# Reading the rows of a scan step for the tensor engine: one full 128-row matmul in place of a 16-row block

## The reference

```
x = x + attention_layer(x, cond)      # B = 8, S = 1024, 512 features, 16 heads
x = x + scan_layer(x, cond)           # d_inner = 1024, d_state = 16

# scan_layer
xr, gate = split(x @ W_in.T);  xr += cond
xc = silu(causal_conv4(xr));   xn = layernorm(xc) * ln_g + ln_b
Bm, Cm, dt = split(xn @ W_xproj.T)
Ad = 1 + tanh(dt @ W_dt.T + b_dt) * 0.01 * (-tanh(A_log))
Bd = Bm * min(norm(xn), 1)
for t in range(S):                    # h: (B, 16, 1024)
    h = clip(h * Ad[t] + Bd[t] * xn[t], -10, 10)
    y[t] = sum over the 16 states of Cm[t] * h
y = (y + D * xn) * silu(gate) @ W_out.T
```

## Time and profile before

| | |
|---|---|
| median of 3 runs | 6766.6 us (6751.14 to 6771.64) |
| the profiled execution | 6754.87 us, span 6753.0 us |
| PE busy (matmul) | 6163.2 us, 91% |
| PE weight loads | 2592.1 us, 38% |
| DVE busy | 4561.2 us, 68% |
| ACT busy | 2370.0 us, 35% |
| POOL busy | 3208.9 us, 48% |
| mean granted TensorE clock | 0.929 of 2.4 GHz |

### The profile page before, as it was taken

The page is one execution under the profiler, slowest core; times in us unless marked ns, Lnnn a source line. Parts: engine busy times, 40 slices in busy tenths (PEclk is TensorE's granted clock), DMA queues, the critical chain, the costliest instruction groups (busy, mean ns, idle before and its releaser), DMA issues. The chain is left out here.

```text
span 6753.0 us, 73075 instructions
## 1 busy us (share of the span) xinstructions
PE 6163.2 (91%) x24000; PEld 2592.1 (38%) x24000; DVE 4561.2 (68%) x5829; ACT 2370.0 (35%) x4476; POOL 3208.9 (48%) x2625
## 2 busy tenths in 40 slices
PE   8999999999999999999855889999999999999997
PEld 3444444444444444444332323333333333333333
DVE  4655555655655655655336888888788888888883
ACT  2443434444444443434443323233232323233110
POOL 1766756757666676755622323324142333424212
PEclk7999999999999999999877779898999989899998
DMA  2223223133232323223032334434344343434433
GB/s 89 77 79 94 79 72 93 53 107 88 71 91 57 93 79 91 82 61 87 30 114 69 80 94 109 116 89 138 78 118 108 105 125 92 130 84 123 102 88 98
DMA packets 411563, 613.08 MB, mean 91 GB/s; under 512 B 58768, under 2 KB 190096, under 8 KB 410672
## 3 DMA queue, kind: packets, MB, share of 16 engines
q1 hardware_dynamic: 374320, 558.04, 30.0%
q10 hardware_dynamic: 36864, 50.38, 3.0%
HBM read 305.12 MB, written 201.38 MB: 75 GB/s over the span
## 5 line engine op out<-in xcount | busy, mean ns | idle before, releaser
L1103 POOL TENSOR_TENSOR acc<-acc,prob 128x512 f32<-128x512 f32 x1536 | 1906.5, 1275 | 962.2 <-PE bank L793 728.6
L1033 DVE TENSOR_REDUCE mx<-bank 128x1 f32<-128x512 f32 x2048 | 1315.5, 685 | 587.9 <-PE bank L763 583.3
L1904 DVE SCALAR_TENSOR_TENSOR g<-xps,bd,g 128x1024 f32<-128x1024 f32 x1024 | 1313.7, 1283 | 295.3 <-PE xps L1667 223.0
L926 ACT ACTIVATE prob<-misc 128x512 f32<-128x512 f32 x1496 | 842.6, 597 | 850.3 <-PE misc L780 686.5
L763 PE MATMUL bank<-khat,qhat 96*128 96x512 f32 x2048 | 989.5, 534 | 39.5 <-DVE mx L1033 20.2
L1910 DVE TENSOR_SCALAR g<-g,lim 128x1024 f32<-128x1024 f32 x1024 | 872.6, 852 | 30.0
L780 PE MATMUL misc<-qhat,khat 98*128 98x512 f32 x1679 | 724.4, 461 | 57.4 <-ACT prob L926 40.9
L1667 PE MATMUL xps<-sx,spread 16*128 16x512 f32 x2048 | 539.0, 529 | 223.9 <-DVE g L1904 208.8
L1682 PE MATMUL yps<-g,cexp 128*32 128x512 f32 x4096 | 667.1, 687 | 1.5 <-DVE g L1910 1.5
L1667 PEld LDWEIGHTS xps<-sx,spread 16*128 16x128 f32 x2048 | 200.5, 195 | 955.8 <-DVE g L1904 547.3
L763 PEld LDWEIGHTS bank<-khat,qhat 96*128 96x128 f32 x2048 | 390.3, 195 | 432.5 <-issue 298.7
(11 more groups left out here) (198 smaller groups left out, 6789.3 us busy)
## 6 DMA issues: line engine op xcount, KB each, us to landing
sx<-scratch_xhl SPq DMA_DIRECT2D x512, 128.0 KB, 5.0
scratch_dx<-dx SPq DMA_DIRECT2D x64, 512.0 KB, 2.8
scratch_xhl<-xhi SPq DMA_DIRECT2D x64, 512.0 KB, 4.4
scratch_xhl<-xn SPq DMA_DIRECT2D x64, 512.0 KB, 4.9
scratch_y<-ysb SPq DMA_DIRECT2D x512, 64.0 KB
dx_t<-scratch_dx SPq DMA_DIRECT2D x59, 512.0 KB, 6.1
y_t<-scratch_y SPq DMA_DIRECT2D x59, 512.0 KB, 4.1
xt_n<-in_x SPq DMA_DIRECT2D x112, 256.0 KB, 2.9
```

The costliest lines, as they stand in the source:

```text
L926: act.activation(to, bank[m][:, 0:QC], ACT.Exp, scale=SCALE).then_inc(sem[f"act_m{m}"], 1)
L1033: dve.tensor_reduce(self.mx2[:, h * TT + qt, c:c + 1], bank[m][:, 0:QC], AX.X, ALU.max).then_inc(sem[f"dve_m{m}"], 1)
L1103: pool.tensor_tensor(self.acc[:, a, h, :], self.acc[:, a, h, :], self.prob[:, (n % 2) * GH + h, :], ALU.add).then_inc(sem["pool_acc"], 1)
L1904: dve.scalar_tensor_tensor(self.g[:, t % 4, :], self.xps[t % 2][:, :], self.bd[:, i % 2, tl:tl + 1], self.g[:, (t - 1) % 4, :], ALU.mult, ...
```

## The change

`spread` becomes four matrices side by side. Matrix j has the old zeros and ones in the rows of block j and zeros in all other rows. Each matmul of "x" now reads all 128 partitions of `sx` and matrix j, so both matmuls of a pair use the full array. Since all rows of `sx` are read, VectorE clears both buffers of `sx` once at the start, and the first two unit loads wait for that. The load and the copy of `spread` are four times as large. The planner and its order stay as they were.

```diff
-        self.spread = sb("spread", [P, P], F32R)
+        self.spread = sb("spread", [P, 4, P], F32R)
...
-        sp.dma_start(self.xn[:, 0, 0:P], d["spread"]).then_inc(sem["ld_spread"], 16)
+        sp.dma_start(self.xn[:, 0, 0:4 * P], d["spread"]).then_inc(sem["ld_spread"], 16)
...
                 if n > 1:
                     w.wait_ge(sem["pe_xps"], plan.after("pe_xps", ("x", (n - 1) * UNIT - 1)))
+                else:
+                    w.wait_ge(sem["dve_set"], 4 + 2 * CT + 3)
...
                 for half in range(2):
-                    j = 2 * part + half
-                    mm = pe.matmul(self.xps[t % 2][:, half * BANK:(half + 1) * BANK],
-                                   self.spread[32 * j:32 * j + 2 * B, :], self.sx[32 * j:32 * j + 2 * B, n % 2, wd, :],
-                                   start=True, stop=True)
+
+                    mm = pe.matmul(self.xps[t % 2][:, half * BANK:(half + 1) * BANK], self.spread[:, 2 * part + half, :],
+                                   self.sx[:, n % 2, wd, :], start=True, stop=True)
...
-        dve.tensor_copy(self.spread[:, :], self.xn[:, 0, 0:P]).then_inc(sem["dve_set"], 1)
+        dve.tensor_copy(self.spread[:, :, :].rearrange("p j m -> p (j m)"), self.xn[:, 0, 0:4 * P]).then_inc(sem["dve_set"], 1)
...
         dve.tensor_scalar(self.a_neg[:, :], self.a_neg[:, :], -1.0, None, ALU.mult).then_inc(sem["dve_set"], 1)
+
+        dve.memset(self.sx[:, :, :, :].rearrange("p s w c -> p (s w c)").bitcast(F32), 0.0).then_inc(sem["dve_set"], 1)
...
     spread = ((r % 32 < 2 * B) & (r % 32 % B == c // NST)).astype(np.float32)
+    spread = np.concatenate([spread * (r // 32 == j) for j in range(4)], axis=1)
```

## The result

The median falls from 6761.3 us (the kernel before, four runs) to 6654.5 us (four runs, 6648.4 to 6658.5): 107 us, a ratio of 0.984 with a 95% interval of 0.9823 to 0.9857. The forecast was 6711 us with a range from 6665 to 6766. Of the 56 us between 6711 and 6654.5, 5 lie in the start of the sum: it began from a median of 6766.6 us of three runs, and with the fourth it is 6761.3.

What follows compares the result with a forecast made beforehand. PE and DVE were taken to be late in turn. Modes -28, clock -29 and set-up +1 gave -56 us, from 6754.9 to 6699 for the profiled execution; 11.7 more for the median made 6711, range 6665 to 6766.

Steps and rivals of the forecast that it cites:

- What bounds the scan: Between 3608 and 6633 us PE and DVE alternate as the late engine; PE is late in 23 of 47 waits.
- The modes: Full-array pairs avoid mode changes against side matmuls: 8.2 us of PE per chunk, 4.0 arriving, 28 us over seven chunks.
- Side, spread, side: A spread pair between two side matmuls on PE: 1.49 us before, 1.29 after, 0.20 saved, 41 times a chunk.
- the neighbourhoods that I costed at nothing: Pairs on PE with "out" before, behind or on both sides, or after waiting: no net cost assumed.
- the pair's 0.21 + 0.21: The pair's two matmuls on PE no longer run side by side and take 0.21 us each, in sequence.
- The clock: More rows in the spread raise PE's granted clock: 0.4 of the half-clock time goes, at 0.15 for each, saving 29 us.
- stretches of the second kind: Stretches with less side work, 4666 to 4749 and 5059 to 5140: 0.15 us lost per us at half clock.
- When the result is there: The spread's result for "q": +0.01 us in a waiting step, unchanged behind side work, 0.21 longer behind "out" or a wait.
- the set-up: Clearing `sx`, the larger load and copy of `spread`, and the new wait at the start: 1 us added.
- The large clock gain: Rival for the whole scan: both gains arrive, 28 us and some 70 to 100, giving 6640 to 6680; chance 0.15.
- Absorbed: Rival: PE's shorter stretches end in longer waits for DVE, clock hardly changes; 0 to -20 us, 6747 to 6767; chance 0.23.
- Slower: Rival: lost concurrency of the pair isn't paid back if weight loads don't hide; 6837 us, or 6983; chance 0.10.

Runs made afterwards that it cites:

- e5_rows32: The changed kernel with the pair back in row blocks of 32, reading all 32 rows of a block, 16 of them zeros: 6717.2 us, ratio 0.9933 against the kernel before.
- e4_k64: The changed kernel with the blocks of `sx` packed without gaps and each spread matmul reading 64 rows, in row blocks of 64: 6838.5 us, ratio 1.0115.
- e3_k65: The changed kernel with the blocks of `sx` packed without gaps and each spread matmul reading 65 rows, still in full mode: 6702.6 us, ratio 0.9917.
- e1_filler: The kernel before, plus one unused 128-row matmul ahead of each pair in the first chunk and the second half of later ones: 6819.7 us, ratio 1.0088.

## Why the prediction went wrong, point by point

**What bounds the scan: right.** PE and DVE take turns at being late, and the gain came where PE was late: DVE's busy time in the scan is the same before and after, and only its idle time fell. The whole scan before, and after:

```profile
3608.00:6633.00 3025.00, 2785.21 (x10747) 1028.46 (x10745) 2596.73 (x2899) 845.73 (x1702) 942.08 (x792) 0.91 0.40 102
```

```profile
3607.00:6530.00 2923.00, 2657.92 (x10746) 1174.84 (x10744) 2597.79 (x2899) 844.48 (x1702) 946.83 (x792) 0.98 0.41 105
```

**The modes: right in kind, too large in size.** Side, spread, side saves 0.17 us (1.49 to 1.32) and not 0.20, and the neighbourhoods that I costed at nothing cost a little: 0.02 to 0.04 us toward "out", and about 0.03 from "out" to a side matmul. What was too small is the pair's 0.21 + 0.21: its two matmuls hold PE for 0.46 us together (0.89 less the 0.43 of the side matmul). By an estimate from these, a chunk saves 41 x 0.17 less some 1.8 us for the others, near 5 us of PE, not 8.2. Half of it over seven chunks is 17 us, not 28. The runs agree: from 32 rows in blocks to 65 in the full mode, with 436 and 424 us at half clock, the medians differ by 15 us, though the intervals of their ratios overlap. The last chunk, at 0.98 in both kernels, lost 4 us.

**The clock: the step that failed.** "I take it that 0.4 of the half-clock time goes", and then "Most half-clock time lies in stretches of the second kind, so I take 0.15". Both were too low. The share stood on 482 us, all but the 77 of the first chunk's end. Of these, 370 went: 0.77. The price, with the estimated 17 us left to the modes, is (107 - 17) / 370 = 0.24 us for each. So the term was about 90 us and not 29. That is 61 us too little, against a saving of 107 where I had 56; the modes, 11 us too large, hid a part of it.

The cause is shown by runs that change the rows alone: 16 to 32 rows in blocks gives 0.8% (1.001 to 0.9933), and 65 to 96 rows in the full mode 26 us with intervals that don't touch. From 65 to 128 rows it is 0.8% (0.9917 to 0.984), with the packing changed too. Together the two steps to 32 and to 128 are 1.54% or 104 us by ratios, and by the medians against 6761 they are 44 and 48 us, 92 together; between these two lies the clock's part, if the packing does nothing. The rest, 3 to 15 us, is the modes'.

The Trainium skill's rule in "TensorE: Matmul & The Clock Gate", Part 1, that activity releases the throttle, agrees so far: with the instructions alike, more rows left 252 us at the lower level in place of 424. It does not speak of rows. "TensorEngine Tiling (Array Packing)", Key Properties, has the drain at a change of mode, and the 0.53 us from the last side matmul to the 64-row pair, where side matmuls follow each other in 0.43, agree with that.

Where was the price wrong? The two kinds of the earlier trace rows are the second and the last 32 steps of a chunk. In the kernel before, the four quarters of the six middle chunks, in order, hold 29, 72, 99 and 147 us at half clock. The third, which the prediction did not price, is worth as much as the second, and the last is worth more than my pair of rows said. Steps 64 to 95 of the chunk from 4360 in the kernel before, and then steps 64 to 95 and 96 to 127 of the same chunk in e5_rows32 (the last ones before are the 83 us at 0.84 of the earlier trace rows):

```profile
4571.00:4666.00 95.00, 88.68 (x384) 36.12 (x382) 83.28 (x102) 30.77 (x51) 38.54 (x30) 0.91 0.41 104
```

```profile
4567.00:4658.00 91.00, 84.28 (x386) 34.61 (x388) 82.96 (x102) 31.27 (x52) 38.25 (x30) 0.96 0.41 107
4658.00:4737.00 79.00, 70.02 (x275) 23.02 (x268) 72.34 (x80) 16.90 (x27) 37.32 (x33) 0.89 0.51 154
```

In each of the two, 4 us went with 9 to 10 us at half clock: 0.4 for each, at the same DVE work within one instruction. Over the last quarters of all middle chunks with row blocks the times scatter, and a straight line through them gives 0.23 for each. The end of the first chunk is worth nothing, as forecast: its last 32 steps take 76.5 to 77.1 us with 16, 32, 65, 96 and 128 rows, and 27 to 77 us of them are at half clock. So of the change's fall, 142 us in the first chunk came with 20 us less time, and 275 us in the middle ones with 78 (the modes' part included). A mean over stretches with different bounds should have been weighed by stretch, and each price taken from more than one pair.

The kernel before shows a price too, by itself. Of the 27 executions beside the variants, the five with the highest mean clocks (0.930 on average) took 6750.1 us on average and the four with the lowest (0.923) 6781.5: some 31 us for 101 us at half clock, 0.3 for each. That these go together does not say which comes first, since longer waits may have lowered the clock; the runs that change the rows do.

**When the result is there; the set-up: right.** The late spreads became fewer, and the clear and the copy lie in DVE's idle time.

**The rivals.** The large clock gain, at 0.15, was the one that came: 6654.5 lies in its 6640 to 6680, in the far half that the range left out, with the clock's part in its 70 to 100 us and the modes' below its 28. "Absorbed" did not: PE's waits for DVE rose by 24 us, not by the whole saving. "Slower" did not either, since the loads hide in the full mode. That e4_k64 ended at 6838 us, beside the 6837 worked out for this rival, is chance: there a pair between side matmuls costs 0.41 us more than in the full mode, where the rival had 0.21, and the cause is two halves in sequence with the mode changes kept.

**Left open.** Which share of the 15 us between e5_rows32 and e3_k65 is mode and which clock isn't resolved, nor what the packing of the blocks does from 96 to 128 rows. Each edit of the rows changes those of the weight load along with those of the matmul, so which of the two counts isn't told apart. Which sums of rows, columns and time the clock's grant follows isn't either: e1_filler streams 128 rows once more and still has 491 us at half clock, the change has 139.

## What to carry to other kernels

Before trading rows for modes, look at the granted clock: where it is low and TensorE is sometimes late, unused rows filled with zeros can be free activity. Try that first within the same block size, since it costs no time on TensorE (0.7% here from 16 rows to 32). Price half-clock time stretch by stretch, by several pairs of stretches with the same work at different clocks, and count nothing where another engine is the bound; an extra matmul that only feeds the clock cost more here than it returned.

## What the runs showed of the hardware

- The number of rows that a matmul reads moves the granted clock between its levels of 1.2 and 2.4 GHz, at the same number of instructions and the same modes: 584 and 436 us at half clock for 16 and 32 rows in row blocks, 424, 252 and 139 for 65, 96 and 128 rows in the full mode (the last with another packing). Zeros and ones in the 64 gap rows do alike (139 and 163 us).
- 64 rows and 65 rows are different modes: side, spread, side takes 1.73 and 1.32 us, and the kernels 6838.5 and 6702.6.
- In a full-mode pair of float32r matmuls of 128x512, each holds the engine for about 0.23 us at the full clock, and both weight loads hide.
